# A cross-attention and FFN kernel: the first layer norm's scaling moves from DVE to ACT, and the loops are written out

## The reference

```python
def _layernorm(x, axis=-1, eps=1e-05):
    ...
    return (x - m) / jnp.sqrt(v + eps)

        q = (query @ Wq + bq).reshape(B, Nq, H, D).transpose(0, 2, 1, 3)
        k = (key_value @ Wk + bk).reshape(B, Nkv, H, D).transpose(0, 2, 1, 3)
        v = (key_value @ Wv + bv).reshape(B, Nkv, H, D).transpose(0, 2, 1, 3)
        attn = jnp.einsum('bhqd,bhkd->bhqk', q, k) * scale
        attn = jnp.clip(attn, -CLAMP, CLAMP)
        attn = jax.nn.softmax(attn, axis=-1)
...
        x = jnp.einsum('bhqk,bhkd->bqhd', attn, v).reshape(B, Nq, Cq)
        return x @ Wo + bo
...
        P = jnp.einsum('bsd,dr->bsr', x, U1)
        H = jax.nn.gelu(jnp.einsum('bsr,rf->bsf', P, V1) + b1)
        Q = jnp.einsum('bsf,fr->bsr', H, U2)
        return jnp.einsum('bsr,rd->bsd', Q, V2) + b2
    x = x + _L0_xattn_ref(_layernorm(x, axis=-1), ctx_768, ...)
    x = x + _L0_ffn_ref(_layernorm(x, axis=-1), ...)
```

## Time and profile before

| what | value |
|---|---|
| time, 3 runs | median 623.55 us (623.04 to 624.56) |
| the profiled execution's own time | 620.38 us |
| its span, first to last instruction | 618.4 us |
| busy: PE, DVE, POOL, ACT | 94%, 80%, 58%, 50% |
| granted TensorE clock, mean | 0.999 |

### The profile page before, as it was taken

The page is one execution under the profiler, slowest core; times in us unless marked ns, Lnnn a source line. Parts: engine busy times, 40 slices in busy tenths (PEclk is TensorE's granted clock), DMA queues, the critical chain, the costliest instruction groups (busy, mean ns, idle before and its releaser), DMA issues.

```text
span 618.4 us, 12409 instructions
## 1 busy us (share of the span) xinstructions
PE 582.5 (94%) x4583; PEld 474.5 (77%) x4583; DVE 495.8 (80%) x706; ACT 310.5 (50%) x505; POOL 356.3 (58%) x250
## 2 busy tenths in 40 slices
PE   7886999999999999999998999898989898989996
PEld 6685887888888888888876677686868686868774
DVE  3589779889888888889679887988888888887664
ACT  1344354444544444535464546656565565656562
POOL 1549656665756665665556465646464738283641
PEclk9999999999999999999999999999999999999999
DMA  8423082303231223112320421212121111201012
GB/s 268 143 66 105 20 272 88 93 29 101 85 102 41 78 88 99 57 64 69 120 70 35 136 56 64 79 59 68 69 69 69 63 56 39 97 17 52 18 51 85
DMA packets 29733, 50.10 MB, mean 81 GB/s; under 512 B 5069, under 2 KB 6783, under 8 KB 29567
## 3 DMA queue, kind: packets, MB, share of 16 engines
q1 hardware_dynamic: 29215, 48.80, 23.8%
q10 hardware_dynamic: 480, 0.80, 0.5%
HBM read 32.49 MB, written 16.78 MB: 80 GB/s over the span
## 4 chain that ended last, share of the span: by engine, by line
PE 70%; DVE 13%; issue 5%; ACT 4%; POOL 3%; DMA 3%; SPq 1%; DVEq 0%; ACTq 0%; POOLq 0%
PE bank L929 40%; PE ps_s L929 10%; PE bank L1026 6%; PE bank L1003 5%; PE ps_s L977 4%; DVE once L770 3%; PE bank L1050 2%; DMA ss<-in_L_xattn_Wv 2%; DVE hs_r L791 2%; DVE hs_r L793 2%; DVE ssum L731 2%; PE bank L951 1%; DVE smax L726 1%; DMA xs<-in_x 1%; DVE ss L717 1%
## 5 line engine op out<-in xcount | busy, mean ns | idle before, releaser
L464 POOL TENSOR_TENSOR hs_r<-ss,hs_r 128x512 fp32r<-128x512 f32 x63 | 84.4, 1340 | 107.1 <-ACT hs_r L631 107.0
L610 ACT ACTIVATE ss<-ps_s,bias_c 128x512 f32<-128x512 f32 x128 | 88.1, 689 | 83.2 <-PE ps_s L929 80.2
L929 PE MATMUL bank<-hs_r,u_r 128*128 128x512 f32 x384 | 111.0, 398 | 14.0 <-DVE hs_r L793 10.5
L390 POOL TENSOR_TENSOR ss<-ss,smax 128x1232 f32<-128x1232 f32 x32 | 75.1, 2346 | 70.0 <-DVE smax L726 69.9
L929 PE MATMUL ps_s<-p1t_r,v_r 128*128 128x512 f32 x384 | 112.4, 401 | 0.7 <-DVE p1t_r L782 0.7
L929 PE MATMUL bank<-zt_r,wqo_r 128*128 128x256 f32 x768 | 99.5, 285 | 0.4 <-DVE zt_r L669 0.4
L929 PEld LDWEIGHTS bank<-hs_r,u_r 128*128 128x128 f32 x384 | 70.9, 188 | 36.4 <-DVE hs_r L793 8.8
L929 PE MATMUL bank<-wqo_r,ot_r 128*128 128x512 f32 x384 | 97.7, 403 | 0.2 <-DVE xs L749 0.2
L929 PEld LDWEIGHTS bank<-zt_r,wqo_r 128*128 128x128 f32 x768 | 93.2, 189 | 1.6 <-issue 1.0
L397 POOL TENSOR_TENSOR ss<-ss,rsum 128x1232 f32<-128x1232 f32 x32 | 72.1, 2253 | 38.6 <-DVE rsum L733 38.6
L929 PEld LDWEIGHTS bank<-wqo_r,ot_r 128*128 128x128 f32 x384 | 69.8, 188 | 15.6 <-issue 0.6
(11 more groups left out here) (89 smaller groups left out, 861.5 us busy)
## 6 DMA issues: line engine op xcount, KB each, us to landing
xs<-in_x SPq DMA_DIRECT2D x64, 256.0 KB, 2.8
y_between<-xs SPq DMA_DIRECT2D x32, 256.0 KB, 2.0
xs<-y_between SPq DMA_DIRECT2D x4, 1024.0 KB, 5.6
fw<-y_between SPq DMA_DIRECT2D x4, 1024.0 KB, 5.6
out<-fw SPq DMA_DIRECT2D x16, 256.0 KB, 2.0
out<-xs SPq DMA_DIRECT2D x16, 256.0 KB, 2.1
ss<-in_L_xattn_Wq SPq DMA_DIRECT2D x2, 512.0 KB, 10.3
xs<-in_L_xattn_Wo SPq DMA_DIRECT2D x1, 1024.0 KB, 10.9
```

The source lines that it names most:

```text
L390: pool.tensor_tensor(heads(sc, k), heads(sc, k), smax[:, k, :].unsqueeze(2).broadcast_to([P, H, KV]), ALU.subtract).then_inc(s_sub, 1)
L464: pool.tensor_tensor(hs[:, c % 4, 1, :], hg[:, c % 4, :], hs[:, c % 4, 0, :].bitcast(F32), ALU.subtract)\
L610: act.activation(hg[:, c % 4, :], ps_s[:, c % 4, :], ACT.Gelu_apprx_tanh, bias=b1_c[:, c:c + 1]).then_inc(h_gelu, 1)
L929: mm = pe.matmul(ps, lhs(a), rhs(c), start=first and i == 0, stop=last and i == len(PASSES) - 1)
```

## The change

`norm_z` goes from DVE's program to ACT's. DVE computed (x − mean) · rstd from the two columns mean and rstd; ACT computes rstd · x + z_shift, one instruction a tile with scale and bias as columns, where z_shift = −mean · rstd is made by POOL in `rstd_of`, with two instructions of one column each and a semaphore of their own, `shift_done`. On ACT the two tiles of z stand behind the first two probability copies of the block (parts 0 and 1 of tile u = 0) and ahead of `q_copy`. The first blocks have places of their own: z of block 0 is ACT's first work, z of block 1 stands behind the first query copy, z of block 2 behind the first exponential. `pairs` no longer makes a loop: every j is written out on every engine, in both stages.

```diff
-def pairs(eng, total, body):
-
-    head, tail = (2, 2) if total > 8 else (1, 1)
-    for j in range(head):
-        body(j)
-    with eng.Fori(head, total // 2 - tail) as j:
-        body(j)
-    for j in range(total // 2 - tail, total // 2 + 1):
+def pairs(total, body):
+
+    for j in range(total // 2 + 1):
         body(j)
...
                 pool.tensor_tensor(rstd[:, 2 * b:2 * b + 2], var_e[:, 2 * b:2 * b + 2], mhalf[:, 0:2],
                                    ALU.pow).then_inc(rstd_done, 1)
+                pool.wait_ge(rstd_done, n + 1)
+                for k in (2 * b, 2 * b + 1):
+                    last = pool.tensor_scalar(z_shift[:, k:k + 1], mv[:, k, 0:1], rstd[:, k:k + 1], -1.0,
+                                              ALU.mult, ALU.mult)
+                last.then_inc(shift_done, 1)
...
+            def norm_z(j, b):
+                n = 2 * j + b
+                act.wait_ge(shift_done, n + 1)
+                for u in range(2):
+                    k = 2 * b + u
+                    until(act, zt_full, 2 * n + u - 1)
+                    act.activation(z[:, u, :], xa[:, k, :], ACT.Identity, bias=z_shift[:, k:k + 1],
+                                   scale=rstd[:, k:k + 1]).then_inc(z_done, 1)
...
+            norm_z(0, 0)
             for half in range(2):
...
             q_copy(0, 0, 0)
+            norm_z(0, 1)
             act.wait_ge(in_wo, 16)
...
                         if before:
                             copy_probs(*shift(j, b, -1), u, (0, 1))
+                        if u == 0 and there(NA, j, b, 2) and not is_block(0, j, b):
+                            norm_z(j + 1, b)
...
                         if u == 0 and there(NA, j, b, 0):
                             exponent(j, b, 0)
+                        if u == 0 and is_block(0, j, b):
+                            norm_z(1, 0)
...
-            def norm_z(j, b):
-                n = 2 * j + b
-                dve.wait_ge(rstd_done, n + 1)
-                for u in range(2):
-                    k = 2 * b + u
-                    until(dve, zt_full, 2 * n + u - 1)
-                    dve.tensor_scalar(z[:, u, :], xa[:, k, :], mv[:, k, 0:1], rstd[:, k:k + 1],
-                                      ALU.subtract, ALU.mult).then_inc(z_done, 1)
...
                 clip(0, 1, 1)
-                norm_z(1, 1)
                 maxima(0, 1, 1)
...
-                        if u == 0 and there(NA, j, b, 2):
-                            norm_z(j + 1, b)
```

More of the change, by code:

```diff
@@ L163, in xattn_ffn @@
         rstd = sb("rstd", [P, 4])
+        z_shift = sb("z_shift", [P, 4])
         smax = sb("smax", [P, 4, H])
@@ L192, in xattn_ffn @@
             sem(n) for n in ("wq_hi", "wq_lo", "wq_lo_pool", "wo_hi", "wo_lo", "pad_zero", "bias_ready"))
-        stats_done, mv_done, var_done, rstd_done, z_done = (
-            sem(n) for n in ("stats_done", "mv_done", "var_done", "rstd_done", "z_done"))
+        stats_done, mv_done, var_done, rstd_done, shift_done, z_done = (
+            sem(n) for n in ("stats_done", "mv_done", "var_done", "rstd_done", "shift_done", "z_done"))
         zt_full, zt_hi, zt_lo, q_full, q_done = (
@@ L329, in body @@
                             sp.dma_start(xb[:, k, :], x_t[row, :, :]).then_inc(in_xb[k], 16)
-            pairs(sp, NA, body)
+            pairs(NA, body)
             for k in range(4):
@@ L347, in body2 @@
                               .then_inc(outs[bb], 16)
-            pairs(sp, NB, body2)
+            pairs(NB, body2)
             for b in range(2):
@@ L437, in body @@
                         rstd_of(*shift(j, b, 3))
-            pairs(pool, NA, body)
+            pairs(NA, body)
             def y_plus_b2(j, b, t):
@@ L470, in body2 @@
                             y_plus_b2(*shift(j, b, 1), c - 12)
-            pairs(pool, NB, body2)
+            pairs(NB, body2)
         @block.scalar
@@ L611, in gelu @@
                                bias=b1_c[:, c:c + 1]).then_inc(h_gelu, 1)
-            pairs(act, NA, body)
+            pairs(NA, body)
             def q2_high(j, b):
@@ L638, in body2 @@
                             p1_high(*shift(j, b, 1))
-            pairs(act, NB, body2)
+            pairs(NB, body2)
         @block.vector
@@ L686, in _ @@
             norm_stats(0, 0, 1)
-            norm_z(0, 0)
             dve.wait_ge(wq_hi, 1)
@@ L701, in _ @@
             norm_stats(0, 1, 1)
-            norm_z(0, 1)
             dve.wait_ge(in_bv, 16)
@@ L802, in first_blocks @@
                 clip(0, 0, 1)
-                norm_z(1, 0)
                 sums(0, 0, 0)
@@ L876, in body @@
                         h_split(0, 0, 0)
-            pairs(dve, NA, body)
+            pairs(NA, body)
             def q2_low(j, b):
@@ L919, in body2 @@
                             p1_low(*shift(j, b, 1))
-            pairs(dve, NB, body2)
+            pairs(NB, body2)
         @block.tensor
@@ L1177, in body @@
                         hidden(0, 0, 3)
-            pairs(pe, NA, body)
+            pairs(NA, body)
             def project_v2(j, b, t):
@@ L1207, in body2 @@
                             project_u1(*shift(j, b, 1))
-            pairs(pe, NB, body2)
+            pairs(NB, body2)
 _NAMES = ["x", "ctx_768", "L0_xattn_Wq", "L0_xattn_bq", "L0_xattn_Wk", "L0_xattn_bk", "L0_xattn_Wv",
```

## The result

| | time, median (lowest to highest) | ratio to before, 95% interval |
|---|---|---|
| before | 623.41 us (620.47 to 625.77) | |
| changed | 625.54 us (624.27 to 627.43) | 1.0038 (1.0023 to 1.0052) |

The account below looks back on a forecast made before the run. PE was taken to bound the middle, so only the first blocks count: 0 for middle and loops, +1.2 us at tile 2's transposes, 623.55 + 1.2 = 624.8 us; range 622.4 to 627.4.

Parts of the forecast that it names:

- The middle: Middle blocks of the first stage: PE is full, so relieving DVE is worth 0; ACT's z pair, 1.4 us, fits 2.21.
- First and second step: First blocks: DVE's sums of tile 0 start 0.56 us earlier; POOL's two shift instructions take 0.45, `shift_done` at 49.5.
- Third to fifth step: Block 1: ACT waits for the shift, delaying z, third copy and PE; tile 2's transposes start at 62.85, 1.2 us later.
- The clock: Rival, chance 0.24: PE's 5.4 us gap in block 1 drops the clock to 1.2 GHz; 2.0 us more, 626.8 us.
- The loops: Writing out the loops, whole kernel: priced at 0 from equal block periods, 0.4 us at most.

Follow-up runs that it names:

- ACT from block 4 on: Changed kernel with z of blocks 0 to 3 back in its old places on DVE: 621.50 us, ratio 0.9971 to before.
- the gap filled: Changed kernel with 40 transposes of the identity added on PE ahead of the transposes of tile 1 in block 1: 622.68 us, ratio 0.9982 to before.
- start-filled kernel: Kernel before with 36 instead of 16 keep-warm matmuls at the start: 622.42 us, ratio 0.998 to before.
- the loops alone: Kernel before with its loops written out and nothing else: 622.14 us, ratio 0.9969; once more, 622.43 us, ratio 0.9988.
- the wait alone: Kernel before, z still on DVE, with one wait added on ACT in block 1 for the rstd of block 3: 624.04 us, ratio 1.0014.
- z moved: Changed kernel with z of block 3 moved behind the third probability copy of tile 0 in block 1: 621.50 us, ratio 0.9961 to before.
- Fillers in three waits: Kernel before, loops out, z on DVE, 36 keep-warm matmuls at the start, 16 identity transposes in block 1, 8 in block 2: 620.56 us, ratio 0.9956.

## Why the prediction was right, point by point

**The middle: right.** 20.12 us a block against 20.13 with DVE 7% of the span freer. (The second stage, which was to keep its 32.3, had 32.37: see the result.) The kernel with ACT from block 4 on agrees, without the first blocks. ACT's pair was said to take 1.4 us; it starts the next instruction 52.31 − 50.88 = 1.43 behind its own start. By the Trainium skill ("ScalarE: Activation LUTs", What ACT_TABLE_LOAD costs), an ACTIVATE takes 186 ns, 0.833 ns for each element of a partition and 93 ns for each column operand; z then comes to 186 + 512 × 0.833 + 2 × 93 = 799 ns as an estimate. The trace agrees, with 805, and my 746 was low.

**First and second step: right.** POOL's normalisation of tile 1 begins 47.07 − 31.17 = 15.90 us behind DVE's first clip; before 46.48 − 30.00 = 16.48 by its timeline. That is 0.58 less, forecast 0.56. The shift pair took 0.50, forecast 0.45. It ended at 50.85, forecast 49.5; of the difference 1.17 is the late start of this execution (31.17 − 30.00), 0.2 the step's.

**Third to fifth step: the right chain, a little too short.** Wait on `z_shift`, z, query copies, third copy, PE, query copies, turned z, tile 2: each row is there, in that order. Counted from POOL's normalisation, tile 2 was to come at 62.85 − 45.92 = 16.93 and came at 17.29 with the clock held (the gap filled). Wait less the first step's gain: forecast 1.2, measured 2.14 − 0.58 = 1.6. Of the difference 0.2 is the shift's; another 0.1 is added on the way from there to PE's transposes of tile 1 (6.48 behind POOL's normalisation, forecast 52.1 − 45.92 = 6.18), and 0.1 between DVE's low part of z and PE's start (64.12 − 58.90 = 5.22, forecast 5.15). One slip of the recorded sum: +0.8 to +2.4 with ±0.3 is 624.05 to 626.25, not 624.2 to 626.0; the range given at its end is wider than either.

**The clock: the rival came true, beside the forecast and not instead of it.** The forecast had set PE's work behind the gap at 0.85 + 3.10 = 3.95 us; in the trace it is (55.13 − 53.54) + 4.95 = 6.54. The rival's price for this was 2.0, with 3.95 at most; measured 2.6. The Trainium skill ("TensorE: Matmul & The Clock Gate", Why this matters for your kernels; the prediction gives the section another name) warns that a gap between bursts of matmuls puts TensorE back to half its clock; the trace agrees here, with 0.50 behind 6.27 us.

**Then why not 626.8 or more?** The corrected wait and the clock give 623.41 + 1.6 + 2.6 = 627.6, and the median is 625.54. Two terms of the sum account for most of the 2.1 between. *The loops, priced at 0 with 0.4 at most*: the spans give 0.5 us back at the end, where the periods that I priced them from could not show it.

*The clock of before, taken as 1.00 everywhere from one profile*: it falls in before too. Not every fall costs: the one behind before's 2.10 us wait, 4.62 instead of 3.10 us of matmuls in the start-filled kernel, moved nothing at tile 2. The one behind tile 2's wait does, by about 1.5 us (57.8 to 58.0 against 56.1 to 56.8). It stands in three profiles, those of the loops alone, the wait alone and z moved, and in neither of the two of the changed kernel, which lost its 2.6 us earlier. If before's median execution has it, 627.6 − 0.5 − 1.5 = 625.6. That second part is argued, not shown: the profile of before is one of the rare ones without a fall, and no run counts where the others have theirs. The mean clocks fit: 0.989 to 0.991 in the three profiles with that fall, 0.989 to 0.990 in the median of before, 0.997 where only the start has one. The point forecast was close by luck: the clock that it left out and the gains that it left out nearly cancelled.

What stays open: why the same wait loses the clock in one execution and not in another, why the changed kernel keeps it at tile 2, and what SyncE does in its last 0.5 us. The changed kernel with its loops kept wasn't tried.

## What to carry to other kernels

When work moves to an engine that has time to spare, look at the first blocks, not at the shares: an instruction that waits is a gate for all that is queued behind it, and here its place, one copy earlier or later, decided the sign (1.0038 against 0.9961). A wait on PE can cost twice, itself and the clock that falls in it (2.14 and 2.60 us here), but only where the work behind it is on the path: elsewhere 1.5 us more of matmuls moved nothing. Fillers in three waits were worth more (0.44% with the loops out) than moving 43 us of work off DVE. And one profiled execution has a clock of its own: compare its mean with that of the timed runs before taking "1.00 in every stretch" as the kernel's.

## What the runs showed of the hardware

- The same wait does not always cost the same. PE stood 2.10 us ahead of the transposes of tile 1 in before, in the kernel with z moved and in that with the start filled; the 24 matmuls behind took 3.10, 3.73 and 4.62 us. At tile 2 they took 4.60 us behind a wait of 1.31 (the wait alone) and 3.10 behind a wait of 1.31 (the changed kernel). Executions of before lie up to 6.7 us apart (619.63 to 626.28 in one comparison), and their spans follow their mean clock in the main: 618.5 to 619.1 us at 0.999, and 621.7 to 623.2 at 0.988; but seven executions at 0.994 have 621.0 to 622.9. In the profiled ones the falls are all in the first 70 us.
- A slow warm-up can help. In the profile of before the 16 keep-warm matmuls took 3.68 us and the wait behind them was 1.85 us, with no fall; in that of the changed kernel the same 16 took 1.97 and the wait was 4.40, with the fall. All profiles with 16 of them go the same way: 3.67 or 3.68 us and no fall at the start in four, 1.96 to 2.56 us and the fall in six. The granted clock reads 1.00 in those first stretches of both profiles, so it does not explain the 3.68 us.
- SyncE's two loops lengthen the span by 0.5 us behind the last matmul, though it only issues DMAs: 44.53 to 44.55 us behind the chain's last group of 15 matmuls in the three profiles that have them, 44.01 to 44.07 in the eleven without.
